# Graph stage: the 64 expert calls move from the gather loop to the end gathers

## The reference, cut to what matters

```
h = (x_flat @ W_gat).reshape(M, HEADS, NUM_EXPERTS)
e = leaky_relu(a_src[src] + a_dst[dst], negative_slope=0.2)
ee = exp(e - segment_max(e, dst)[dst])
alpha = ee / (segment_sum(ee, dst)[dst] + 1e-16)
agg = segment_sum(h[src] * alpha[:, :, None], dst) + b_gat
scores = layernorm(agg) averaged over the heads      # one score per node and expert
topk_s, topk_i = top_k(scores, 2);  w = softmax(topk_s)
for ei in range(4):
    hh = gelu(x @ W1[ei] + b1[ei])
    out = out + g[ei] * (hh @ W2[ei] + b2[ei])        # g from w and topk_i
```

## Time and profile before

| | us |
|---|---|
| median of 3 runs (10416.91 to 10425.58) | 10419.22 |
| the profiled execution, its own time | 10424.57 |
| its span | 10422.8 |
| PE busy | 8047.6 (77%) |
| DVE busy | 7616.0 (73%) |
| POOL busy | 6807.3 (65%) |
| ACT busy | 5297.9 (51%) |

### The profile page before, as it was taken

The page is one execution under the profiler, slowest core; times in us unless marked ns, Lnnn a source line. Parts: engine busy times, 40 slices in busy tenths (PEclk is TensorE's granted clock), DMA queues, the critical chain, the costliest instruction groups (busy, mean ns, idle before and its releaser), DMA issues. The chain is left out here.

```text
span 10422.8 us, 111413 instructions
## 1 busy us (share of the span) xinstructions
PE 8047.6 (77%) x34183; PEld 3953.7 (38%) x34183; DVE 7616.0 (73%) x6810; ACT 5297.9 (51%) x6228; POOL 6807.3 (65%) x3866
## 2 busy tenths in 40 slices
PE   0168888888888888888888787899389999970769
PEld 0123333333333333333333332333167777750532
DVE  8769999999999999999999833677354444443144
ACT  0056666666666666666666422576245555540123
POOL 0059999999999999999999744100276666644047
PEclk8589999999999999999999987899699999985579
DMA  0066666666666666676666610000222222210022
GB/s 10 0 150 178 177 179 178 177 179 178 177 180 176 177 182 174 177 184 174 177 182 175 172 9 6 6 1 1 12 37 24 23 23 24 22 20 7 0 68 89
DMA packets 385894, 1064.91 MB, mean 102 GB/s; under 512 B 106435, under 2 KB 129603, under 8 KB 383379
## 3 DMA queue, kind: packets, MB, share of 16 engines
q1 hardware_dynamic: 338482, 1044.16, 38.2%
q0 software_dynamic: 47136, 17.04, 3.6%
HBM read 995.98 MB, written 63.50 MB: 102 GB/s over the span
## 5 line engine op out<-in xcount | busy, mean ns | idle before, releaser
L535 POOL TENSOR_TENSOR hC<-h,Cb 128x1024 f32<-128x1024 f32 x1536 | 3602.0, 2359 | 430.1 <-DVE h L630 411.5
L630 DVE TENSOR_TENSOR_SCAN h<-dA,B_ps 128x1024 f32<-128x1024 f32 x1344 | 3073.2, 2287 | 156.4
L308 PE MATMUL y_ps<-hC,con 128*128 128x512 f32 x6144 | 2967.7, 606 | 81.8 <-DVE gz L636 80.3
L455 ACT ACTIVATE dA<-delta,negA 128x1024 f32<-128x1024 f32 x1344 | 1535.4, 1145 | 1207.4 <-DVE h L630 1204.1
L616 DVE TENSOR_TENSOR B_ps<-dx,B_ps 128x1024 f32<-128x1024 f32 x1344 | 1624.0, 1208 | 161.0 <-PE B_ps L302 161.0
L308 PEld LDWEIGHTS y_ps<-hC,con 128*128 128x128 f32 x6144 | 1185.4, 194 | 1146.8 <-issue 943.0
L2637 POOL DMA_INDIRECT g_got<-scratch_node,g_idx x1152 | 1121.3, 973 | 582.0 <-issue 335.3
L302 PE MATMUL B_ps<-Bpart,sel 96*128 96x512 bf16 x2688 | 828.2, 390 | 648.5 <-DVE h L630 646.2
L2684 PE MATMUL g_pick<-g_third,g_hot 128*128 128x256 bf16 x10752 | 1255.9, 274 | 50.4 <-DVE g_got L2814 50.4
L2684 PEld LDWEIGHTS g_pick<-g_third,g_hot 128*128 128x128 bf16 x10752 | 1020.3, 98 | 284.7 <-DVE g_got L2814 115.7
L2809 DVE COPY_PREDICATED g_pick<-g_bits,g_pick 128x512 f32<-128x512 int32 (+3 forms) x896 | 369.4, 412 | 847.0 <-PE g_pick L2684 824.0
(11 more groups left out here) (493 smaller groups left out, 11499.6 us busy)
## 6 DMA issues: line engine op xcount, KB each, us to landing
Cb<-scratch_c_rows SPq DMA_DIRECT2D x3072, 256.0 KB, 4.0
drive<-scratch_c_rows SPq DMA_DIRECT2D x384, 256.0 KB, 5.2
eb_share<-scratch_gate_rows SPq DMA_DIRECT2D x128, 256.0 KB, 3.4
scratch_c_rows<-BCrow SPq DMA_DIRECT2D x96, 256.0 KB, 4.0
scratch_edge<-g_out SPq DMA_DIRECT2D x64, 384.0 KB
par<-in_ssm SPq DMA_DIRECT2D x48, 395.5 KB, 5.2
g_got<-scratch_node,g_idx POOLq DMA_INDIRECT x1152, 2.6
scratch_place<-s_zero SPq DMA_DIRECT2D x4, 1024.0 KB, 11.0
```

The source lines that it names most:

```text
L308: last = nc.tensor.matmul(y_ps[:, hs], con[:, K_ID:K_ID + P], hC[k % DEEP][:, hs], start=(k == 0), stop=(k == STEPS - 1))
L455: A(dA[k % DEEP][:, :], delta[d][:, :], ACT.Exp, scale=negA[:, n:n + 1]).then_inc(decay_ready, 1)
L535: G.tensor_tensor(hC[k % DEEP][:, :], hst[k % DEEP][:, :], Cb[k % DEEP][:, :], ALU.mult).then_inc(prod_ready, 1)
L630: V.tensor_tensor_scan(hst[k % DEEP][:, ::step], decayed[:, ::step], driven[:, ::step], 0.0, ALU.mult, ALU.add).then_inc(scanned, 1)
```

## The change

- The expert weights, hid and all expert code leave the gather loop: hidden() and from_hidden() on PE, the Gelu on ACT, keep_experts() on DVE, the weight loads on SP, and the waits for them on PE, ACT and DVE. fill_at and pick_at no longer count them, so the turns of the PSUM banks and of the pick buffers shift.
- In the end block there are new lists for SP (four weight loads) and PE, and additions to ACT's and DVE's. hid, the PSUM bank of the hidden layer and that of the result are doubled. POOL's list there is as before.
- Semaphores are merged: codes_kept and opened become prepared in the gather loop, last_of becomes a second count of apart in the sorting stage, exp_in becomes one more link in the carry block.

The core of the diff (the removed parts first; renamed semaphores are left out):

```diff
-                    for dst, given in zip((win, wout, b1, b2), experts):
-                        sp.dma_start(whole(dst), given).then_inc(w_loaded, 16)
...
-                    if s == 2 and c >= 0:
-                        fill_at["hidden", c] = len(fill_at)
...
-                    if s == 3 and c >= 0:
-                        pick_at["experts", c] = len(pick_at)
...
-                            if s == 2 and c >= 0:
-                                hidden(c)
...
-                            if s == 3 and c >= 0:
-                                from_hidden(c)
...
-                            if s == 2 and c >= 0:
-                                A(hid[:, :], full("hidden", c)[:, :], ACT.Gelu, bias=b1[:, c % GATES:c % GATES + 1]).then_inc(emptied, 1)
...
-                        if c >= 0:
-                            keep_experts(c)
```

```diff
+            hid = [sb(f"hid{k}", [P, HALF]) for k in range(2)]
+            ps_h = [ctx.enter_context(nc.psum_tensor(f"j_ps_h{k}", [P, HALF], fp32)) for k in range(2)]
+            ps_y = [ctx.enter_context(nc.psum_tensor(f"j_ps_y{k}", [P, HALF], fp32)) for k in range(2)]
...
+                @block.sync
+                def _(sp):
+                    for dst, given in zip((win, wout, b1, b2), experts):
+                        sp.dma_start(whole(dst), given).then_inc(w_loaded, 16)
+
+                @block.tensor
+                def _(pe):
+                    def hidden(c):
+                        if c >= 2:
+                            pe.wait_ge(hid_ready, c - 1)
+                        nc.tensor.matmul(ps_h[c % 2][:, :], win[:, c % GATES, :], tnT_sb[:, c // GATES * HALF:(c // GATES + 1) * HALF],
+                                         start=True, stop=True).then_inc(h_ready, 1)
+
+                    pe.wait_ge(w_loaded, 64)
+                    hidden(0)
+                    for c in range(CALLS):
+                        if c + 1 < CALLS:
+                            hidden(c + 1)
+                        pe.wait_ge(hid_ready, c + 1)
+                        if c >= 2:
+                            pe.wait_ge(y_kept, c - 1)
+                        for g in range(GROUP):
+                            last = nc.tensor.matmul(ps_y[c % 2][:, g * C:(g + 1) * C], hid[c % 2][:, g * P:(g + 1) * P],
+                                                    wout[:, c % GATES, :], start=True, stop=True)
+                        last.then_inc(y_ready, 1)
...
                 @block.scalar
                 def _(act):
+                    act.wait_ge(w_loaded, 64)
+                    for c in range(CALLS):
+                        act.wait_ge(h_ready, c + 1)
+                        if c >= 2:
+                            act.wait_ge(y_ready, c - 1)
+                        nc.scalar.activation(hid[c % 2][:, :], ps_h[c % 2][:, :], ACT.Gelu,
+                                             bias=b1[:, c % GATES:c % GATES + 1]).then_inc(hid_ready, 1)
                     nc.scalar.preload_act_table_set("natural_log_exp_and_others")
...
                     link_(V.scalar_tensor_tensor(whole(es), whole(es), 0.2, whole(es), ALU.mult, ALU.max))
+                    for c in range(CALLS):
+                        turn, ex = c // GATES, c % GATES
+                        dve.wait_ge(y_ready, c + 1)
+                        TT(y_all[:, turn * GROUP:(turn + 1) * GROUP, ex * C:(ex + 1) * C],
+                           ps_y[c % 2][:, 0:GROUP * C].rearrange("p (g c) -> p g c", g=GROUP),
+                           b2[:, ex, :].unsqueeze(1).broadcast_to([P, GROUP, C]), ALU.add).then_inc(y_kept, 1)
+                    dve.wait_ge(y_kept, CALLS)
                     dve.wait_ge(taken, 16 * 2 * TILES)
```

More of the change, by code:

```diff
@@ L2117, in sort_stage @@
             sem(n) for n in ("loaded", "link", "turned", "copied", "shifted", "placed", "stored"))
-        apart, last_of = sem("apart"), sem("last_of")
+        apart = sem("apart")
         BLOCKS = ECOLS // P
@@ L2152, in _ @@
                 sp.dma_start(roots_d, ed[1:P:2, ECOLS - 1:ECOLS]).then_inc(stored, 16)
-                sp.wait_ge(last_of, 1)
+                sp.wait_ge(apart, 2)
                 sp.dma_start(branches_d, es2[:, :]).then_inc(stored, 16)
@@ L2243, in _ @@
                 dve.wait_ge(apart, 1)
-                V.tensor_copy(es2[:, :], ed[:, FAN - 1:ECOLS:FAN]).then_inc(last_of, 1)
+                V.tensor_copy(es2[:, :], ed[:, FAN - 1:ECOLS:FAN]).then_inc(apart, 1)
                 dve.wait_ge(placed, 16)
@@ L2550, in graph_stage @@
             pick_ps = [ctx.enter_context(nc.psum_tensor(f"g2_pick{k}", [P, L], fp32)) for k in range(2)]
[L2551 to L2555, removed]
+            loaded, codes_loaded = sem("loaded"), sem("codes_loaded")
             idx_here = [sem(f"idx_here{k}") for k in range(2)]
-            codes_kept, opened, link = sem("codes_kept"), sem("opened"), sem("link")
+            prepared, link = sem("prepared"), sem("link")
             gathered = [sem(f"gathered{k}") for k in range(GOTS)]
@@ L2599, in graph_stage @@
                     if s % 2 and c + 1 < CHUNKS:
[L2600 to L2602 removed]
+                        pick_at[c + 1, s // 2] = len(pick_at)
             with nc.Block() as block:
@@ L2675, in pick @@
                         q, h = s // 2, s % 2
-                        at, ones = pick_at["rows", c, q], hot[pair_no(c, s) % 2]
+                        at, ones = pick_at[c, q], hot[pair_no(c, s) % 2]
                         if h == 0 and at >= 2:
@@ L2688, in pick @@
                             last.then_inc(picked, 1)
[L2690 to L2704, removed]
+                    pe.wait_ge(prepared, 2)
                     turn_flags(0)
-                    pe.wait_ge(codes_kept, 5)
+                    pe.wait_ge(prepared, 5)
                     match(0, 0)
@@ L2743, in keep_match @@
                               full("match", (c, s), half)[:, :], ACT.Relu).then_inc(emptied, 1)
-                    act.wait_ge(w_loaded, 64)
                     keep_spots(0)
-                    act.wait_ge(codes_kept, 2)
+                    act.wait_ge(prepared, 2)
                     keep_match(0, 0)
@@ L2754, in _ @@
                             if s == 1 and c == -1:
-                                act.wait_ge(opened, 1)
+                                act.wait_ge(prepared, 6)
                                 spread_penalty(0)
@@ L2802, in choose @@
                     def choose(c, q):
-                        at = pick_at["rows", c, q]
+                        at = pick_at[c, q]
                         four = pick_ps[at % 2][:, :].rearrange("p (k r f) -> p k r f", k=DEPTH_G, r=RESTS)
@@ L2862, in sums @@
                         ready()
[L2864 to L2869, removed]
                     own(V.memset(flags[:, :, :], 0.0))
@@ L2876, in _ @@
                     set_flags(0)
[L2877 to L2880, removed]
+                    V.tensor_copy(codes[:, :, :].rearrange("p v e -> p (v e)"), staged[:, 0:VARIANTS * P]).then_inc(prepared, 1)
+                    V.tensor_copy(ident[:, :], staged[:, VARIANTS * P:(VARIANTS + 1) * P]).then_inc(prepared, 1)
+                    V.tensor_copy(whole(third[0]), whole(feat)).then_inc(prepared, 1)
+                    dve.wait_ge(prepared, 3)
                     own(V.tensor_tensor(rest, whole(feat), whole(third[0]), ALU.subtract))
                     ready()
-                    V.tensor_copy(whole(third[1]), rest).then_inc(codes_kept, 1)
-                    dve.wait_ge(codes_kept, 4)
+                    V.tensor_copy(whole(third[1]), rest).then_inc(prepared, 1)
+                    dve.wait_ge(prepared, 4)
                     own(V.tensor_tensor(rest, rest, whole(third[1]), ALU.subtract))
                     ready()
-                    V.tensor_copy(whole(third[2]), rest).then_inc(codes_kept, 1)
-                    dve.wait_ge(codes_kept, 5)
+                    V.tensor_copy(whole(third[2]), rest).then_inc(prepared, 1)
+                    dve.wait_ge(prepared, 5)
                     own(V.memset(e[:, :, 0:1], -BIG))
```

17 lines of the change are left out of this document (9 added, 8 removed).

## The result

The changed kernel takes 10280.45 us (median of 4 runs, 10275.87 to 10284.15), the kernel before, run beside it on the same chip, 10422.4 (4 runs, 10416.91 to 10428.84): a ratio of 0.9863, with a 95% interval of 0.9846 to 0.988. The forecast was 10254, the range 10225 to 10290. The profiled execution of after took 10284.15, 140.4 less than the one of before. That splits into three stretches of the two traces: ahead of the graph stage 6.7 us more (the stage starts at 7460.69 instead of 7454.04), the graph stage 145.2 less (7460.69 to 9408.31 against 7454.04 to 9546.86), and behind it 1.9 less.

What follows compares the result with a forecast made beforehand. PE was taken to bound the gather loop and POOL's gathers the end. From 10424.6, less 228.1 (loop) and 0.5 (start), plus 63.0 (end), came 10259.0; 5.4 lower for the median, 10254 us, range 10225 to 10290.

Steps and rivals of the forecast that it cites:

- the third pair's wait: Gather loop, third long match-and-pick pair of a chunk: the pick's 0.80 us wait for DVE goes, saving 0.85 per chunk.
- the period of a call: End block: one expert call takes 3.65 us at the low clock, between 3.44 and 3.73; 64 calls take 233.6.
- the sign of being right: End block: calls every 3.5 to 3.8 us, with PE at clock 0.50 and full, would show the forecast right.
- its allowance of 0.3 for the handovers: End block: the range allows up to 0.3 us more per call for handovers, beyond the period's bounds.
- its pair: Gather loop, second long match-and-pick pair, holding from_hidden(): without it 0.93 us saved per chunk, 4.89 becoming 3.96.
- The 8 us allowed: Gather loop: 8 us each way for such things as lighter DVE and ACT work and ACT's tight pair.
- the 2 us of slack per two chunks: Gather loop: POOL's 36 gathers take 45.1 us against PE's 47.1, so POOL stays just under PE, still waiting for DVE.
- the Gelu table: End block: ACT loads it while the expert weights come in, costing zero; if uncovered, 1.3 us.
- the clock: End block: PE's clock stays at 0.50 throughout the 64 calls, as in earlier busy stretches.
- A: End block: the clock rises, the gathers set the end, and the time is 10191 us; chance 0.11.
- B: POOL bounds the loop (10359 us; sign: no waits for DVE) or new calls don't overlap (10381); together 0.06.
- C: End block: gathers and calls disturb each other, one gather per call, 10483 us; sign: gathers slower than 1.31; chance 0.01.

Runs made afterwards that it cites:

- e4: The changed kernel with the calls in pairs on PE (two hidden(), then two from_hidden(); four hid buffers, four hidden banks): 10266.17 us, ratio 0.9843 to the kernel before.
- e7: The changed kernel with hidden() over 128 rows, the upper 64 rows of weights and features zero, no burst: 10201.72 us, ratio 0.9786 to the kernel before.
- e5: The changed kernel with eight 128-row, 512-column matmuls between hidden(1) and from_hidden(0), covering the Gelu table load: 10201.17 us, ratio 0.9783 to the kernel before.
- e1: The changed kernel with four 128-row, 512-column matmuls on PE while the expert weights come in: 10276.16 us, ratio 0.9855 to the kernel before.
- e8: The changed kernel with paired calls, each pair's second hidden() on copies in rows 64 to 127: 10189.7 us (three runs), ratio 0.9772 to the kernel before.
- e3: The changed kernel without the 64 expert calls, y_all zeroed by DVE, so the experts are left out: 10202.27 us, ratio 0.9783 to the kernel before.
- e9: e1's kernel with a small Gelu on ACT at the end block's start, so the table loads early: 10192.33 us, ratio 0.9783 to the kernel before.
- e2: The changed kernel with e1's burst of four 512-column matmuls, but over 64 rows instead of 128: 10283.08 us, ratio 0.9861 to the kernel before.

## Why the prediction was right, and where it was off

**Right, the sum's shape.** PE bounded the loop and the end became PE's, as the earlier trace rows had it: the third pair's wait went, turn_flags' stayed, no other engine stepped in, and the loads were in after 3.9 us. The median came out 26 us above the forecast and within its range. In the profiled execution it is 25.2 (10284.15 for 10259.0): 15.8 in the end block, 4.0 in the loop, 0.2 at the stage's start, and 5.2 that no term was meant to hold, 6.7 of them ahead of the stage.

**Off, the period of a call: 3.90 for 3.65.** This is the mis-sized term, 0.25 x 64 = 16 us. I bounded a call by equal matmuls in a row and by from_hidden() with its drain, so 3.65 held only 0.21 for two changes of shape, and 3.90 lies outside the 3.5 to 3.8 that I had named as the sign of being right. e4 measured them: 0.24 each, 0.48 per call, on top of 3.42. The range took this in, by its allowance of 0.3 for the handovers; the value did not. What I had called a handover "behind a semaphore" is no wait that the profile shows: PE has no idle time there, and e4, with as many waits per call, halves only the changes. The rows have a part in it: with 128 in both kinds (e7 against e5) a call at the high clock is 0.34 shorter.

**Off, the loop: 224.1 for 228.1.** from_hidden() kept PE for 0.93 between two starts, but without it its pair is only 0.84 shorter (4.89 to 4.05); 0.08 x 63 = 5 us. The 8 us allowed cover it. POOL was also read wrongly: it was to go on waiting for DVE, but its gathers took 1.277 us each instead of 1.251, and its waits went to nothing. So it was nearer to being the bound than the 2 us of slack per two chunks said: 36 gathers take 46.0 of the 47.25.

**Off, the Gelu table.** It was to load while the weights come in. ACT loaded it behind the first hidden(), and PE waited 0.41, too little to matter; but behind e1's burst the same order left PE idle for 1.26 and cost the clock.

**Right, the clock, though the reason was incomplete.** 0.50 throughout was read off, and after shows it over 230 us. I named two causes in one breath, the 64 rows and the 64 columns between weight loads. The first is shown to count: e7 changes the rows alone, and the 64-column matmuls then run at 1.00. The second isn't refuted: in e7 the clock rose behind the 512-column matmuls, and in e4 two from_hidden() in a row, 3.6 us of matmuls with 128 rows and 64 columns each time, left it at 0.50 for 200 us. Whether such narrow ones alone would ever raise it was not run.

The Trainium skill (TensorE: Matmul & The Clock Gate, "Part 1: The HAM clock gate") has the gate open after a sustained busy stretch. The trace of after, busy 230 us at 0.50, does not agree; e7, e8 and the bursts of e1 and e5, busy with 128-row matmuls or with both halves of the rows, do. By the rule alone the changed kernel would have been at the floor of e3, and it was 80 us above: the measurement decides.

**Rivals.** A (clock up, 10191) did not occur in the changed kernel, but its time is what e5 to e9 reach: 10190 to 10204. So its working was right, and only its condition was not met. B did not occur, though the sign that I named for it, POOL without waits in the loop, did: POOL that waits for nothing bounds only if its gathers are waited for, and DVE, which uses them, waited 0.2 us in the whole loop. That was a badly chosen sign. C did not occur; the gathers keep their 1.31 us.

**Not settled.** The runs do not tell how long PE may idle before a raised clock falls: 0.41 us was harmless (e7, e8), 1.26 was not (e1), behind different matmuls. The 6.7 us ahead of the stage lie in unchanged code: the sorting stage, the only one there with an edit, is over 1.7 us sooner in after (the next stage's first load is at 564.00 against 565.66). Other kernels of this study start the graph stage between 7440.1 and 7462.6; I take the 6.7 us for variation between executions, which is not shown.

## What to carry to other kernels

Work that is moved from a busy stretch into a quiet one is paid at the clock that it finds there: price it at the low clock, and then ask what would raise it. Here calls with 64-row matmuls never did in 230 us, and with 64 rows of zeros beside those 64 the first two hidden() raised it within 4 us, at no cost in their own time; e7 is some 220 us faster than before (ratio 0.9786, 0.9769 to 0.9802) where the change alone gave 142. Once the clock is up, look for the first idle time of PE, such as a table load on ACT.

## What the runs showed of the hardware

- Matmuls over 64 and over 128 rows take the same time (3.78 us for four records of 512 columns, float32, in after and e7), but only those over 128 raised the clock: e1's burst of 5.9 us did, e2's of 7.2 us did not.
- Matmuls of 64 columns over 128 rows, 3.6 us in a row in every pair of calls, did not raise it in 200 us (e4).
- A change between the 64-row, 512-column and the 128-row, 64-column matmul costs 0.24 us at 0.50 (e4); at 1.00, making the rows equal saves 0.34 per call, 0.17 per change (e5 against e7).
- Two 64-row matmuls on different halves of the rows run at once: eight records in 3.78 us (e8).
- A raised clock is held for 120 us and more (e5, e9) by the same calls that did not raise it in 230 us (after).
- 1.26 us in which PE stood idle behind the first 64-row matmuls were followed by the fall of a raised clock some 2 us after PE went on (e1); without them it held (e9).
